# Attention with a pruned context and a gated feed-forward: two PSUM banks for the value products' output, two in place of three for the scores

## The chip, the cores and the metric

One NeuronCore of a Trainium2 chip runs the whole kernel. The metric is the device time of one execution in microseconds (us). TensorE is called PE, VectorE DVE, ScalarE ACT, GpSimd POOL, and SyncE, which issues the transfers, SP.

## What is computed

The input `x` has 8 batches of 512 tokens with 128 channels, in float32. The reference, cut to what matters:

```python
xn  = layernorm(x)
q, k, v = split(xn @ w_attn.T + b_attn)          # 16 heads of 8
att = q @ k.T / sqrt(8), causal
S   = relu(att of head 0), first column and diagonal 0
FF  = cumsum over queries of S, shifted by one    # how far a key is to be forgotten
att = att - FF;  keep = the 102 smallest FF of a row, and the diagonal
att = where(keep, att, -inf)                      # one mask for all 16 heads
attn = (softmax(att) @ v) @ w_proj.T + b_proj
ffn  = sum over 8 experts: gate_e * (relu(xn@wi.T + bi + (xn@A_e.T)@B_e.T) @ wo.T + bo)   # top 2
out  = x + attn + ffn
```

## The kernel before, in words

A first block prepares the weights and the first batch. The second block has 8 steps, one for each batch. A step attends over its own batch (`k`) and at the same time prepares the next one (layer norm, q and k, the forgetting sums of head 0, the search for the 102 smallest, the mask). These preparations are spread over the same time slots.

**Units.** The 512 queries of a batch are four tiles `a` of 128, and tile `a` attends to `a+1` blocks of 128 keys. A unit is the work on up to 512 columns of scores: units 0 to 3 of a step are tile 0 with four heads each, 4 to 11 tile 1 with two heads each, 12 to 27 tile 2 with one head, 28 to 43 tile 3 with one head. So a step has `NU` = 44 units, and there are 352 in all. The text names a unit by its number in the step ("unit 43 of step 3").

**A unit's way.** PE computes the scores into a bank `ps_s` (`score`, line 798). DVE adds the mask, writes the sum to `ar` in SBUF and takes the greatest of each row (`mx`, line 1156). POOL subtracts (line 506). PE transposes the result into a bank `ps_t` (`turn`, line 809). ACT takes the exponential into `pr` (line 657). PE multiplies it with the values into the bank `ps_o` (`weigh`, line 825), for four heads at a time (a group). When all 16 heads of a tile are summed, ACT copies `ps_o` to `out_t` (line 666), PE transposes that (the job `ot0` to `ot3`, line 771), DVE divides by the sum, and the projection follows.

**Order.** Each engine runs one fixed program over the slots `t` = 0, 1, 2 ... In slot `t` PE does the jobs that a table gives for the slot (`fill`: the feed-forward part, the preparations, `ot`, `yt`, `proj`), then `score(t)`, `turn(t-3)` and, where unit `t-4` ends a group, `weigh(t-4)`. DVE does its part of the slot's jobs, the masking of unit `t`, and then a part of the search for the next batch. PE works in order, so that a wait of `score` also holds back the `turn` and `weigh` behind it.

**Rings.** PSUM has eight banks: three for the scores (`NS_RING`), two for the transposes, one for the value products, two for all other jobs (`ps_m`). `score(u)` may begin when unit `u-3` is masked (semaphore `masked`). The first group of a tile may begin when ACT has copied the tile before (semaphore `taken`). DVE adds 1 to `masked` with the instruction that reads the accumulator, at the end of each head.

**The stacks.** The scores are computed in bfloat16 from q and k that are split in three parts, which lie as stacks of 96 rows (`qs`, `ks`), a copy for the current step and one for the next. SP copies the parts into the stacks by 12 transfers of 128 KB in SBUF (line 388, `make_stacks`). The stacks of the next batch overwrite those of the step before, so SP waits for the last score of that step first:

```python
sp.wait_ge(scored, NU * n)      # all scores of the steps before n are computed
```

The first reader of the new stacks is the job `s0` (slot 13 of a step, line 729), which computes head 0 of the next batch: it waits on PE for all 12 transfers. The jobs `ot3` (slot 5 of the next step) and `gate` (slot 43) also play a part below.

Of the kernel before, what the change touches and what calls it, by code (L numbers as in the profile page):

```python
# [23 lines left out]
ACT = mybir.ActivationFunctionType  # L24
AX = mybir.AxisListType.X

P = 128
# [4 lines left out]
NA = T // P  # L32
# [17 lines left out]
OW = 512 // NH  # L50
# [12 lines left out]
OFF = [P * a * (a + 1) // 2 for a in range(NA + 1)]  # L63
FOFF = [sum(T - P * x for x in range(c)) for c in range(NA + 1)]

NS_RING, NT_RING, NM_RING = 3, 2, 2
NA_RING, NP_RING = 6, 6
LAG_T, LAG_P = 3, 4
OUT_LAG, OT_LAG, YT_LAG = 1, 2, 4
# [89 lines left out]
def build(nc, x, w_attn, b_attn, w_proj, b_proj, wi, bi, wo, bo, lora_a, lora_b, gate_w, gate_b, out):  # L159
    ctx = ExitStack()  # L160
    with ctx:
        def sb(name, shape, dt=F32):
            return ctx.enter_context(nc.sbuf_tensor(name, shape, dt))
# [106 lines left out]
        out_t = sb("out_t", [P, T])  # L270
# [4 lines left out]
        def bank(name):  # L275
            return ctx.enter_context(nc.psum_tensor(name, [P, 512], F32))

        ps_s = [bank(f"ps_s{i}") for i in range(NS_RING)]
        ps_t = [bank(f"ps_t{i}") for i in range(NT_RING)]
        ps_o = bank("ps_o")  # L280
        ps_m = [bank(f"ps_m{i}") for i in range(NM_RING)]

        names = ["w_in", "x_in", "const", "w_prep", "scored", "masked", "shifted", "turned", "weighed",
# [8 lines left out]
        weighed, summed, taken = s["weighed"], s["summed"], s["taken"]  # L292
# [13 lines left out]
        def run_block(steps, preps, setup=False):  # L306
# [12 lines left out]
            def wait_full(eng, name, k):  # L319

                eng.wait_ge(m_full, full(name, k))
# [13 lines left out]
            with nc.Block() as block:  # L335
# [185 lines left out]
                def _(act):  # L521
# [78 lines left out]
                    for t in range(end):  # L600
                        k, o = divmod(t, NU)
                        for name, n in plan.at.get(t, []):
# [10 lines left out]
                            elif name in ("q", "k"):  # L613
                                j = ("q", "k").index(name)
# [9 lines left out]
                            elif name[0] == "s":  # L624

                                j = int(name[1])
# [11 lines left out]
                            elif name[0] == "h":  # L638
                                f, j = int(name[1]), int(name[2])
# [4 lines left out]
                            elif name[0:2] == "yt":  # L644
                                a = int(name[2])
# [4 lines left out]
                        if 0 <= u < NU * steps:  # L650

                            a, h0, g = UNITS[u % NU]
# [6 lines left out]
                        for kk in range(steps):  # L659
                            for a in range(NA):  # L660
                                if t == NU * kk + LAST[a] + LAG_P + OUT_LAG:

                                    act.wait_ge(summed, NG * kk + GROUPS * (a + 1))
                                    if NA * kk + a >= 1:
                                        wait_full(act, f"ot{(a + 3) % NA}", kk - (a < 1))
                                    nc.scalar.activation(out_t[:, :], ps_o[:, :], ACT.Identity).then_inc(taken, 1)  # L666
                        for n in range(preps + 1):
                            act_prepares(n, t)

# [1 line left out]
                def _(pe):  # L671
# [141 lines left out]
                    def weigh(u):  # L813
                        k, o = divmod(u, NU)
                        a, h0, g = UNITS[o]
                        group = GROUP_OF[o] % GROUPS
                        pe.wait_ge(weighed, u + 1)
                        if group == 0 and NA * k + a >= 1:
                            pe.wait_ge(taken, NA * k + a)
                        for c in range(a + 1):  # L820
                            for j in range(QUAD):
                                hh = QUAD * group + j
                                unit, at = PLACE_OF[a, hh]
                                at = P * (at + c)
                                last = nc.tensor.matmul(ps_o[OW * j:OW * j + OW, P * group:P * group + P],  # L825
                                                        va[:, k % 2, c, VW * hh:VW * hh + OW],
                                                        pr[:, (NU * k + unit) % NP_RING, at:at + P],
                                                        start=(c == 0), stop=(c == a))
                        last.then_inc(summed, 1)

                    for t in range(end):
                        for name, n in plan.at.get(t, []):
                            fill(name, n)
                        if t < NU * steps:
                            score(t)
                        if 0 <= t - LAG_T < NU * steps:
                            turn(t - LAG_T)
                        if 0 <= t - LAG_P < NU * steps and ENDS_GROUP[(t - LAG_P) % NU]:
                            weigh(t - LAG_P)
# [384 lines left out]
```

## Time and profile before

| | |
|---|---|
| median of 3 runs | 806.2 us (805.84 to 806.38) |
| the profiled execution | 806.93 us |
| its span, first to last instruction | 804.7 us |
| mean granted clock of TensorE | 0.904 of full speed |
| busy: PE, DVE, POOL, ACT | 588.6, 551.2, 439.9, 388.0 us |

The span lacks 2.2 us of the execution's time, which lie before the first and behind the last instruction. No engine is busy for more than 73% of the span, so the time is set by the waits between them, and by different ones in different parts of a step. The times of the rows are counted from the start of the span. A timeline row has the start, the duration, the engine (PEld is the loading of weights, which runs ahead of the PE row with the same line), the line of the kernel and the operation; in brackets stands the idle time before it and what ended it.

### The profile page before, as it was taken

Reading aid. Unit: us, or ns where it says so; the run is one execution under the profiler, and the core shown is the slowest. Engines: PE = TensorE matmul, PEld = TensorE weight load, DVE = VectorE, ACT = ScalarE, POOL = GpSimd, SP = SyncE. Lnnn points to the kernel's source line nnn. Section 1 sums busy time; section 2 is a strip of 40 time slices with the busy share of each in tenths; the row PEclk is TensorE's granted clock in tenths of the full one; section 3 lists DMA queues with packets and bytes.
Section 4 is the critical chain, followed back from the end, with each engine's and each line's share of the span. In section 5 each row is a group of like instructions: output and inputs, shape, how many; then the busy total and the mean of one; then the engine's idle time right before and its main releaser. Section 6 shows DMA issues by size and latency. Waiting matters only on the chain. (4 is left out here: it accounts for less than half of the span.)

```text
span 804.7 us, 16830 instructions
## 1 busy us (share of the span) xinstructions
PE 588.6 (73%) x5478; PEld 401.1 (50%) x5478; DVE 551.2 (69%) x2257; ACT 388.0 (48%) x806; POOL 439.9 (55%) x739
## 2 busy tenths in 40 slices
PE   4133038888688787878887888877787868878995
PEld 2111025466446564555555655655456555656574
DVE  6656426598648984699458985699459964797352
ACT  4124105564446554565456555555446454635543
POOL 4321226547755584547655685558554675439552
PEclk9555559998999999999899999999999999989998
DMA  3502230002500051003400050004200150000000
GB/s 82 67 12 28 27 52 1 1 2 38 69 1 2 7 77 25 1 1 46 62 1 1 20 76 14 2 2 62 32 2 2 33 61 2 1 7 9 1 2 14
DMA packets 27286, 18.98 MB, mean 24 GB/s; under 512 B 5417, under 2 KB 27072, under 8 KB 27200
## 3 DMA queue, kind: packets, MB, share of 16 engines
q1 hardware_dynamic: 27200, 17.91, 15.3%
q8 instruction: 45, 0.74, 0.4%
q14 instruction: 41, 0.34, 0.2%
HBM read 3.22 MB, written 2.10 MB: 7 GB/s over the span
## 5 line engine op out<-in xcount | busy, mean ns | idle before, releaser
L506 POOL TENSOR_SCALAR ar<-ar,mx 128x512 f32<-128x512 f32 (+3 forms) x512 | 285.6, 568 | 284.5 <-DVE mx L1156 283.5
L1156 DVE CUSTOM_DVE_ANT_0 ar<-ps_s,mask 128x512 f32<-128x512 f32 (+3 forms) x512 | 232.6, 484 | 109.0 <-PE ps_s L798 106.2
L657 ACT ACTIVATE pr<-ps_t 128x512 f32<-128x512 f32 (+1 forms) x352 | 192.3, 554 | 136.5 <-PE ps_t L809 132.1
L809 PE MATMUL ps_t<-ident,ar 128*128 128x128 f32 x1280 | 205.5, 279 | 26.1 <-ACT pr L657 13.7
L809 PEld LDWEIGHTS ps_t<-ident,ar 128*128 128x128 f32 x1280 | 157.7, 144 | 70.5 <-POOL ar L506 43.1
L798 PE MATMUL ps_s<-ks,qs 96*128 96x512 bf16 (+3 forms) x512 | 131.1, 309 | 45.4 <-PEq L1195 38.1
L825 PE MATMUL ps_o<-pr,va 128*32 128x128 f32 x2560 | 103.3, 292 | 22.6 <-ACT out_t L666 14.8
L825 PEld LDWEIGHTS ps_o<-pr,va 128*32 128x32 f32 x2560 | 66.3, 114 | 47.4 <-ACT pr L657 32.5
L798 PEld LDWEIGHTS ps_s<-ks,qs 96*128 96x128 bf16 x512 | 46.7, 104 | 75.3 <-issue 57.8
L642 ACT ACTIVATE h<-ps_m,bi_col 128x512 f32<-128x512 f32 x64 | 43.8, 685 | 73.2 <-PE ps_m L756 73.2
L756 PE MATMUL ps_m<-zm,b_t 128*128 128x512 f32 x128 | 70.5, 634 | 5.5 <-ACT h L642 4.5
L596 ACT ACTIVATE junk<-nf,cut 128x384 bf16<-128x384 f32 x64 | 42.2, 662 | 25.2 <-POOL nf L483 13.3
L1106 DVE TENSOR_SCALAR_CACHE_REDUCE nf<-ps_m 128x128 f32<-128x128 f32 (+3 forms) x32 | 15.7, 490 | 41.3 <-PE ps_m L740 40.9
L1156 DVE DVE_READ_ACCUMULATOR2_ANT mx<- 128x1 f32 x512 | 41.9, 82 | 0.0
L752 PE MATMUL ps_m<-xnt,wi_t 128*128 128x512 f32 x64 | 39.5, 702 | 3.0 <-DVE va L1092 3.0
L517 POOL TENSOR_TENSOR hsum<-h 128x512 f32<-128x512 f32 x32 | 40.6, 1268 | 0.0
L756 PEld LDWEIGHTS ps_m<-zm,b_t 128*128 128x128 f32 x128 | 23.0, 199 | 29.9 <-issue 24.8
L951 DVE TENSOR_TENSOR_SCAN ft<-ones,s 128x511 f32<-128x511 f32 (+3 forms) x32 | 26.3, 822 | 13.6 <-POOL s L477 12.1
L771 PE MATMUL ps_m<-ident,out_t 128*128 128x128 f32 x128 | 20.0, 279 | 18.7 <-ACT out_t L666 18.7
L632 ACT ACTIVATE s<-ps_m,not_first 128x512 f32<-128x512 f32 (+3 forms) x32 | 16.6, 525 | 35.0 <-PE ps_m L729 35.0
L729 PE MATMUL ps_m<-qs,ks 96*128 96x512 bf16 (+3 forms) x32 | 10.2, 325 | 31.1 <-DMA ks<-parts 25.1
L765 PE MATMUL ps_m<-wo_t,hsum 128*128 128x128 f32 x256 | 31.2, 275 | 0.0
(172 smaller groups left out, 817.4 us busy)
## 6 DMA issues: line engine op xcount, KB each, us to landing
qs<-parts SPq DMA_DIRECT2D x48, 128.0 KB
ks<-parts SPq DMA_DIRECT2D x48, 128.0 KB
xs<-in_L_attn_x SPq DMA_DIRECT2D x8, 256.0 KB, 5.2
out<-res SPq DMA_DIRECT2D x8, 192.0 KB, 2.1
out<-res SPq DMA_DIRECT2D x8, 64.0 KB, 7.9
ar<-in_L_ffn_wi SPq DMA_DIRECT2D x1, 256.0 KB
ar<-in_L_ffn_wo SPq DMA_DIRECT2D x1, 256.0 KB
ar<-in_L_ffn_lora_B SPq DMA_DIRECT2D x4, 64.0 KB
```

The source lines that it names most:

```text
L506: nc.gpsimd.tensor_scalar(col, col, -1.0, mx[:, t % NA_RING, j:j + 1], ALU.mult, ALU.add)\
L517: nc.gpsimd.tensor_tensor(hsum[:, f, :], h[:, 2 * (f % 2), :], h[:, 2 * (f % 2) + 1, :], ALU.add).then_inc(h_sum, 1)
L596: nc.scalar.activation(junk[:, a - 2, 0:P * (a + 1)], nf[:, OFF[a]:OFF[a + 1]], ACT.Sign, bias=cut[:, a:a + 1], scale=-1.0, accum_out=abov ...
L642: nc.scalar.activation(h[:, 2 * (f % 2) + j, :], m[:, :], ACT.Relu, bias=bi_col[:, f:f + 1])\
L657: nc.scalar.activation(pr[:, u % NP_RING, 0:w], ps_t[u % NT_RING][:, 0:w], ACT.Exp, scale=-1.0)\
L752: nc.tensor.matmul(m[:, :], wi_t[:, P * f:P * f + P], xnt[:, n % 2, :], start=True, stop=False)
L756: last = nc.tensor.matmul(m[:, :], b_t[:, P * f:P * f + P], zm[:, j, :], start=False, stop=True, skip_group_check=(j == 1))
L765: last = nc.tensor.matmul(m[:, P * a:P * a + P], hsum[:, f, P * a:P * a + P], wo_t[:, f, :], start=False, stop=(a == hi - 1 and f == NF - 1))
L798: last = nc.tensor.matmul(ps_s[u % NS_RING][:, w * j:w * j + w], qs[:, k % 2, h0 + j, P * a:P * a + P], ks[:, k % 2, h0 + j, 0:w], start=T ...
L809: last = nc.tensor.transpose(ps_t[u % NT_RING][:, P * j:P * j + P], ar[:, u % NA_RING, P * j:P * j + P], ident[:, :])
L825: last = nc.tensor.matmul(ps_o[OW * j:OW * j + OW, P * group:P * group + P], va[:, k % 2, c, VW * hh:VW * hh + OW], pr[:, (NU * k + unit) ...
L1156: nc.vector.tensor_tensor_reduce(out=ar[:, t % NA_RING, w * j:w * j + w], in0=ps_s[t % NS_RING][:, w * j:w * j + w], in1=mask[:, k % 2, OF ...
```

## The change

Two banks instead of one take the output of the value products, used in turn by tile. To make room for the second, the scores get two banks instead of three. No instruction is added or taken away, and each engine runs the same instructions in the same order as before; only what two kinds of instruction on PE wait for is changed. `score(u)` now waits until unit `u-2` is masked. The first group of a tile now waits for ACT's copy of the tile before the last.

```diff
-NS_RING, NT_RING, NM_RING = 3, 2, 2
+NS_RING, NT_RING, NM_RING, NO_RING = 2, 2, 2, 2
...
-        ps_o = bank("ps_o")
+        ps_o = [bank(f"ps_o{i}") for i in range(NO_RING)]
...
-                                    nc.scalar.activation(out_t[:, :], ps_o[:, :], ACT.Identity).then_inc(taken, 1)
+                                    nc.scalar.activation(out_t[:, :], ps_o[(NA * kk + a) % NO_RING][:, :], ACT.Identity).then_inc(taken, 1)
...
-                        if group == 0 and NA * k + a >= 1:
-                            pe.wait_ge(taken, NA * k + a)
+                        tile = NA * k + a
+                        if group == 0 and tile >= NO_RING:
+                            pe.wait_ge(taken, tile - NO_RING + 1)
...
-                                last = nc.tensor.matmul(ps_o[OW * j:OW * j + OW, P * group:P * group + P],
+                                last = nc.tensor.matmul(ps_o[tile % NO_RING][OW * j:OW * j + OW, P * group:P * group + P],
```

## Rows read from the trace of the kernel before

**Rows 1.** The page, first part: an engine's busy time, share of the span, instructions.

```profile
PE 588.6 (73%) x5478; PEld 401.1 (50%) x5478; DVE 551.2 (69%) x2257; ACT 388.0 (48%) x806; POOL 439.9 (55%) x739
```

**Rows 2.** Waits of PE, whole span: who waited for whom, us, times, longest.

```profile
PE ps_m L729 <- DMA ks<-parts: 25.1, 7, 8.4
...
PE ps_o L825 <- ACT out_t L666: 14.8, 7, 2.3
...
PE ps_s L798 <- DVE mx L1156: 7.2, 8, 0.9
```

**Rows 3.** Timeline of all engines, the start of step 4 (slots 1 to 5).

```profile
464.66 0.08 DVE L1156 DVE_READ_ACCUMULATOR2_ANT mx<- 128x1 f32 x1
...
464.80 0.23 PEld L798 LDWEIGHTS ps_s<-ks,qs 96*128 96x128 bf16 x4 [0.29 <-DVE mx L1156]
...
465.51 0.29 DVE L1156 CUSTOM_DVE_ANT_0 ar<-ps_s,mask 128x128 f32<-128x128 f32 x1
...
468.78 0.15 PEld L798 LDWEIGHTS ps_s<-ks,qs 96*128 96x128 bf16 x2
...
470.26 0.08 DVE L1156 DVE_READ_ACCUMULATOR2_ANT mx<- 128x1 f32 x1
...
471.19 0.59 ACT L666 ACTIVATE out_t<-ps_o 128x512 f32<-128x512 f32 x1
...
471.92 0.43 PE L825 MATMUL ps_o<-pr,va 128*32 128x128 f32 x8 [2.26 <-ACT out_t L666]
472.27 0.42 PEld L771 LDWEIGHTS ps_m<-ident,out_t 128*128 128x128 f32 x4 [0.20 <-issue]
```

**Rows 4.** Timeline of SP: first stack transfers, ends of steps 3, 4 and 5.

```profile
460.13 3.88 SPq L388 DMA_DIRECT2D qs<-parts  x6
...
547.35 3.88 SPq L388 DMA_DIRECT2D qs<-parts  x6
...
636.64 3.88 SPq L388 DMA_DIRECT2D qs<-parts  x6
```

**Rows 5.** Timeline of PE around job s0 of step 4.

```profile
485.99 0.38 PE L729 MATMUL ps_m<-qs,ks 96*128 96x512 bf16 x1 [1.44 <-DMA ks<-parts]
...
487.47 1.13 PE L752 MATMUL ps_m<-xnt,wi_t 128*128 128x512 f32 x2
```

**Rows 6.** Timeline of PE, job s0 of step 5.

```profile
573.59 0.38 PE L729 MATMUL ps_m<-qs,ks 96*128 96x512 bf16 x1 [3.33 <-DMA ks<-parts]
```

**Rows 7.** Line 729 from 200 to 700 us: PE's idle time before it, times.

```profile
  DMA ks<-parts: 16.7, 6
```

**Rows 8.** Timeline at the end of step 3, units 42 and 43.

```profile
458.07 0.10 PEld L798 LDWEIGHTS ps_s<-ks,qs 96*128 96x128 bf16 x1
...
458.81 0.97 PEld L722 LDWEIGHTS ps_m<-gate_t,xnt 128*128 128x128 f32 x8
...
459.28 0.09 DVE L1156 DVE_READ_ACCUMULATOR2_ANT mx<- 128x1 f32 x1
...
459.62 0.18 PEld L798 LDWEIGHTS ps_s<-ks,qs 96*128 96x128 bf16 x1
...
461.63 0.08 DVE L1156 DVE_READ_ACCUMULATOR2_ANT mx<- 128x1 f32 x1
```

**Rows 9.** Timeline at the end of step 0, unit 43's score, unit 41's masking.

```profile
192.08 0.29 PEld L798 LDWEIGHTS ps_s<-ks,qs 96*128 96x128 bf16 x1
...
192.99 0.08 DVE L1156 DVE_READ_ACCUMULATOR2_ANT mx<- 128x1 f32 x1
```

**Rows 10.** The same at the end of step 5.

```profile
636.12 0.18 PEld L798 LDWEIGHTS ps_s<-ks,qs 96*128 96x128 bf16 x1
...
638.13 0.08 DVE L1156 DVE_READ_ACCUMULATOR2_ANT mx<- 128x1 f32 x1
```

**Rows 11.** Windows from s0 to s1, steps 4 and 5: busy times, PEclk, DMA share, GB/s.

```profile
485.99:489.29 3.30, 3.30 (x26) 1.75 (x27) 0.56 (x2) 1.20 (x2) 0.83 (x2) 1.00 0.00 0
573.59:578.52 4.93, 4.93 (x27) 2.17 (x28) 0.57 (x2) 1.20 (x2) 0.83 (x2) 0.67 0.00 0
```

## The prediction

> **What bounds the kernel now.** I read the page first: no engine is full (PE 73%, DVE 69%, [rows 1]), so the question is which wait ends last in each part of a step. Then the waits of PE [rows 2]. Two of them name the buffers of this change: the first value product of a tile waits for ACT's copy `out_t` 7 times, 14.8 us in all, and the scores wait for DVE's masking only 8 times, 7.2 us. Read alone, this says that the value products need the bank and the scores can spare one. The third row, job s0 waiting for the stack transfers, 25.1 us, decides whether that is so.
>
> So next the timeline at the start of a step [rows 3]. All 7 waits for `out_t` are at the first tile of a new step: the group of unit 0 is held until the last tile of the step before is copied (2.26 us, until 471.92). Right behind it in PE's program is job ot3, which transposes that same copy and needs it anyway.
>
> Then SP's timeline [rows 4] and PE at s0. At the end of a step SP waits for unit 43's score and issues the 12 stack transfers at once; s0 waits for the last of them. In step 4 the first is issued at 460.13 [rows 4] and s0 starts at 485.99 [rows 5], 25.86 us later. Of these PE sits idle for the last 1.44 us [rows 5]; in step 5 for the last 3.33 us [rows 6]. Line 729 shows such a wait six times from 200 to 700 us, 16.7 us in all [rows 7], one for each of steps 1 to 6. So the first part of these six steps is set by the transfers, not by PE: whatever PE gains or loses between slot 0 and slot 12 vanishes in this wait, up to its length, and whatever moves **unit 43's score** moves s0 and all behind it.
>
> **The value products' second bank.** It takes away the 2.26 us wait at each start of a step, so that the group of unit 0 (0.35 us from its row to that of ot3, 471.92 to 472.27, [rows 3]) can run while PE waits for the copy. The wait itself goes to ot3. Without any other effect ot3 would start 0.35 us earlier. In six of the seven places the wait for the transfers stands behind it, so it is worth 0 there; where that cover fails it is worth 0.35 us a step. At the other tiles' starts, ot0 to ot2, which need the copy themselves, already come ahead of the next tile's first group in PE's program; nothing is to be had there.
>
> The Trainium skill (Perfetto Trace Analysis, "Matmuls") says that independent groups of matmuls should go through different PSUM banks, so that one's evacuation overlaps the next one's matmuls. By that rule the 14.8 us of rows 2 would be the gain; the trace agrees that the wait is there, but shows the reader of the evacuated data next in line.
>
> **The scores' lost bank: the first-order cost on PE.** `score(u)` must now wait for the masking of unit u-2. I set each score's load in the trace against the end of that masking. In slots 8 to 25 the masking is always done well before, and the ring of two costs nothing. In slots 26 to 43 and 0 to 7, where DVE also searches for the next batch, it is often late. Most of this is not lost: DVE sets the pace there, and a score that comes late still comes before DVE needs it. Tightest is unit 1 of a step: in step 4 the masking it must now follow ends at 464.74 and DVE begins on unit 1 at 465.51 [rows 3]. A wait for `mx` took 0.06 us to release PE (464.74 to 464.80, [rows 3]); four matmuls and their latency take some 0.5 us, so DVE is late by 0 to 0.3 us. At slot 4 the score, before at 468.78, must wait for unit 2's masking, which ends at 470.34 [rows 3], and holds back turn(1), the exponential of unit 1 and with it `out_t`. The score itself is 1.62 us late (470.40 against 468.78); between turn and exponential ACT's other work leaves about 1 us that takes up part of it. My estimate is that `out_t` starts some 0.6 us later than 471.19, and ot3, with the 0.35 us gained, 0.2 to 0.5 us later. In steps 1 to 6 the wait for transfers hides this; in step 7, where nothing is prepared, there is no such wait: **0.4 us**.
>
> **The scores' lost bank: the transfers.** Here the late score is not hidden. At the end of step 3, unit 43's score started loading at 459.62 and SP issued at 460.13. It must now follow unit 41's masking, which ends at 461.71 (461.63 + 0.08): 2.09 us late, with the 0.06 us of release 2.15 [rows 8]. Could PE's own work make it later still? Unit 42's score, before at 458.07, follows unit 40's masking (459.37) at 459.43; from unit 42's score to unit 43's PE needed 1.55 us (turn, and the `gate` job of 0.97 us), so PE is ready at 460.98, before 461.71: DVE decides. The distance is the same at the end of step 5: 636.12 against 638.21, 2.09 us [rows 10]. At the end of step 0 it is 192.08 against 193.07, 0.99 us [rows 9]. The ends of steps 0 to 5 trigger the six waited transfers. DVE's masking of unit 41 comes after the search's last rounds and does not itself move by the late scores; POOL's and ACT's preparations of `parts` are done before.
>
> Sum: 0.99 + 5 x 2.09 + 6 x 0.06 = **11.8 us**. Does it all arrive? s0 starts when the last transfer lands, in all six steps; the transfers take the same time from a later start; PE's arrival at s0 moves by 0.5 us at most, against idle times of 1.44 us and more. Behind s0 PE is busy without a gap (3.30 of 3.30 us, [rows 11]), and then DVE sets the pace on data that come from s0. So each step is longer by the full amount. The Trainium skill (DMA: Bandwidth & Descriptors, "Rules for kernel authors") asks to issue a transfer early and wait for it late; the change issues it later with the wait where it was, and by that rule too the time is longer.
>
> **The clock.** From s0 to s1 the same work takes 3.30 us in step 4, at a granted clock of 1.00 (2.4 GHz), and 4.93 us in step 5, at 0.67, a mean of 2.4 and 1.2 GHz [rows 11]. What PE did before: it was idle for 1.44 us in step 4 and 3.33 us in step 5 [rows 5, 6]. After the change step 4's idle time is near 1.44 + 2.15 - 0.4 = 3.2 us, like that of step 5 before, so I expect the slow stretch there too: 4.93 - 3.30 = **1.6 us**. The others have theirs already; a longer idle time might lengthen it. Bounds: nothing (the slow stretch may even begin while PE is idle), and above a second one in each step, 6 x 1.63 = 9.8 us. I take nothing, since the rows know one only.
>
> **The sum against the profiled execution:** 806.93 + 11.8 + 1.6 + 0.4 = 820.7 us. That execution is 0.7 us above the median shown, so for a median I say **820.0 us**, 1.7% slower.
>
> **Rivals.**
>
> *The second bank pays.* If the 14.8 us of rows 2 were on the path, the time would be 806.2 - 14.8 = 791.4 us. For it: the size of the wait and the ring's good record, 8 waits only. Against: ot3 behind it and the idle time before s0. It decides only if s0 no longer waits for the transfers and ot3 is not held by `out_t`. Chance 4%.
>
> *The late trigger is absorbed*, because the chain from s0 to the end of the step has 2 us of room that a wait elsewhere hides: then 806 us, perhaps 0.35 us less for each start. Against: from s0 to the next step's first issue step 4 took 61.36 us (485.99 to 547.35) and step 5 63.05 us (573.59 to 636.64, [rows 4 to 6]); the 1.63 us that step 4 was quicker just behind s0 [rows 11] were still there at its end, so what happens at s0 comes through. Chance 3%. A part absorbed, as when DVE reaches unit 41 earlier: 811 to 816 us, 7%.
>
> *The scores' waits cost more than the trigger.* PE is late all through slots 26 to 43; if DVE or ACT is held there (feed-forward, turn and exponential stand behind the waiting score), each step loses more: 0.3 us at unit 1 and up to the second slow stretch of 1.63 us, so up to 6 x 1.9 = 11.6 us more, 832 us. For it: many scores wait; against: DVE has room at all but one of them. Chance 16%.
>
> The forecast has the remaining 70%, with a range of its own of 817.5 to 823. A measurement of this kernel tells about 0.2% (1.6 us) from no change: the runs shown spread over 0.07%, and that has to hold on another chip too. Faster: 4%. Same: 3%. Slower: 93%. The range for 8 in 10 is 815.5 to 826: it takes in half of the clock's upper bound and the upper edge of the partial case.
>
> **What the changed kernel's profile would show.** (1) The wait of the value products for `out_t` gone, and ot3 waiting for `out_t` at each start of a step instead, about 2 us. (2) Unit 43's score waiting for `mx`, and SP's first issue 2.1 us closer to the masking of unit 41 and later in its step. (3) From issue to s0 still 26 us, with PE idle there for 3 to 5.3 us in each of steps 1 to 6: some 28 us in all in place of 16.7. (4) Each step about 2.15 us longer from one first issue to the next (step 4: 3.8). (5) The score's waits for `mx` grown from 7.2 us to tens of us, while DVE's busy time and the time from s0 to unit 41's masking stay within 0.5 us (step 4: plus 1.6). If (3) shows a smaller idle time, the trigger is not the cause; if (5) fails, the third rival is right.

## The result, and the profile after

| | before | after |
|---|---|---|
| median | 806.0 us (802.5 to 806.4, 4 runs) | 815.5 us (811.0 to 818.4, 4 runs) |
| the profiled execution | 806.93 us | 818.4 us |
| its span | 804.7 us | 816.2 us |
| granted clock, mean | 0.904 | 0.900 |

The changed kernel is slower: ratio 1.0131, 95% interval 1.0096 to 1.0166. In the later comparisons the kernel before ran between 798.1 and 813.4 us with medians of 804.9, 805.7 and 805.0, so one execution says less than the first three runs let one think. Here and in the experiments a few executions ran in a second, slower state, whatever the kernel; the ratios leave them out, the medians and ranges do not.

The waits of PE in the changed kernel, against [rows 2]:

```profile
PE ps_s L798 <- DVE mx L1157: 48.9, 66, 1.6
...
PE ps_m L729 <- DMA ks<-parts: 32.3, 7, 8.3
PE ps_m L771 <- ACT out_t L666: 19.6, 18, 1.3
...
PE ps_m L771 <- DVE zm L1117: 5.5, 6, 0.9
```

The value products (now line 826) no longer wait for `out_t`: the 14.8 us are gone from the list. The scores' waits have grown from 7.2 to 48.9 us, and the wait of s0 for the transfers, from 25.1 to 32.3 us. The busy times are those of before (PE 588.9, DVE 551.2, against [rows 1]).

The end of step 3, where [rows 8] stood (unit 43's score, the masking it follows, and the transfers that follow it):

```profile
464.19 0.08 DVE L1157 DVE_READ_ACCUMULATOR2_ANT mx<- 128x1 f32 x1
...
464.32 0.10 PEld L798 LDWEIGHTS ps_s<-ks,qs 96*128 96x128 bf16 x1 [0.82 <-DVE mx L1157]
464.33 0.39 PE L798 MATMUL ps_s<-ks,qs 96*128 96x512 bf16 x1 [0.73 <-DVE mx L1157]
...
464.75 1.28 SPq L388 DMA_DIRECT2D qs<-parts  x2
```

Unit 41 is masked at 464.27, the score's load starts 0.05 us later and SP issues 0.43 us after that. Before, SP's first issue came 1.58 us ahead of the end of that masking (460.13 against 461.71, [rows 8]); now it comes 0.48 us behind it. That is the 2.1 us.

The start of step 3, slots 4 and 5, in place of [rows 3]:

```profile
386.46 0.08 DVE L1157 DVE_READ_ACCUMULATOR2_ANT mx<- 128x1 f32 x1
...
386.60 0.39 PE L798 MATMUL ps_s<-ks,qs 96*128 96x256 bf16 x2 [1.40 <-DVE mx L1157]
...
387.36 0.43 PE L826 MATMUL ps_o<-pr,va 128*32 128x128 f32 x8
...
387.96 0.59 ACT L666 ACTIVATE out_t<-ps_o 128x512 f32<-128x512 f32 x1
...
388.70 0.63 PE L771 MATMUL ps_m<-ident,out_t 128*128 128x128 f32 x4 [0.91 <-DVE zm L1117]
```

The wait of 2.26 us for `out_t` is now two others: 1.40 us of the score of unit 4 for the masking of unit 2, and 0.91 us of ot3, which the profile puts down to DVE; `out_t` itself ends only 0.15 us before ot3 starts. From the end of unit 41's masking to ot3 it is 10.79 us (377.91, from its row at 377.83, to 388.70); before, in the same step, it was 10.55 us (372.42 to 382.97). At four more of the seven starts it is the same 10.8 us (at that of step 4 a slow stretch makes it 12.5). The late score costs more than the second bank gains, and the difference is 0.24 us; experiment 1 tells the two apart. The last start, that of step 7, is another matter: 10.47 us against 8.66.

SP's first issue at the ends of steps 3 to 5, in place of [rows 4]:

```profile
464.75 3.89 SPq L388 DMA_DIRECT2D qs<-parts  x6
...
552.43 3.88 SPq L388 DMA_DIRECT2D qs<-parts  x6
...
644.90 3.88 SPq L388 DMA_DIRECT2D qs<-parts  x6
```

PE at s0 of steps 3 to 5, in place of [rows 5, 6]:

```profile
401.30 0.38 PE L729 MATMUL ps_m<-qs,ks 96*128 96x512 bf16 x1 [1.83 <-DMA ks<-parts]
```

```profile
488.99 0.38 PE L729 MATMUL ps_m<-qs,ks 96*128 96x512 bf16 x1 [1.42 <-DMA ks<-parts]
```

```profile
578.61 0.58 PE L729 MATMUL ps_m<-qs,ks 96*128 96x512 bf16 x1 [5.11 <-DMA ks<-parts]
```

And the windows from s0 to s1 of steps 1, 3, 4 and 5 (columns as in [rows 11]; the eighth figure is the granted clock):

```profile
219.93:226.21 6.28, 6.28 (x27) 2.91 (x28) 0.57 (x2) 1.28 (x2) 0.83 (x2) 0.50 0.01 3
401.30:404.60 3.30, 3.30 (x27) 1.74 (x28) 0.56 (x2) 1.20 (x2) 0.83 (x2) 1.00 0.02 5
488.99:492.29 3.30, 3.30 (x26) 1.75 (x27) 0.57 (x2) 1.20 (x2) 0.83 (x2) 1.00 0.01 3
578.61:584.75 6.14, 6.14 (x27) 2.91 (x28) 0.57 (x2) 1.28 (x2) 0.83 (x2) 0.51 0.00 0
```

After the long idle times the whole stretch runs at 1.2 GHz (6.1 to 6.3 us), where before a part of it did (4.9 us); after the two short ones it runs at 2.4 GHz.

**Where the 11.5 us of the two profiled executions lie.** The first issue of a step and the start of s0 cut each step in two:

| step | issue to s0, before | after | s0 to the next issue, before | after |
|---|---|---|---|---|
| 1 | 25.7 | 26.8 | 63.1 | 66.4 |
| 2 | 26.2 | 25.6 | 63.0 | 66.5 |
| 3 | 26.3 | 22.9 | 62.9 | 63.5 |
| 4 | 25.9 | 24.2 | 61.4 | 63.4 |
| 5 | 26.2 | 26.2 | 63.1 | 66.3 |
| 6 | 26.2 | 26.4 | (end of span: 141.8) | (144.9) |

The first issue of step 1 came 0.2 us later. From issue to s0 all six together are 4.4 us *shorter*, from s0 to the next issue the five stretches are 12.6 us longer, and from the last s0 to the end it is 3.1 us: 0.2 - 4.4 + 12.6 + 3.1 = 11.5 us. Step 4 shows the pure price, since neither kernel has a slow stretch behind s0 there: 63.4 against 61.4 us, **2.1 us** unrounded, as predicted. The rest of the 12.6 us, 2.2 us, is the clock: 1.2 to 1.4 us more in each of steps 1, 2 and 5, and 1.6 us less in step 3, which lost its slow stretch.

The 3.1 us after the last s0 have no waited transfer behind them. About 0.9 us is again the slow stretch behind s0 of step 6. The other 2.2 us lie at the start of step 7: from the end of unit 41's masking to the end of unit 4's in the next step it is 9.95 us (735.20 to 745.15) against 7.78 (725.84 to 733.62). The first part of both stretches, up to DVE's start on unit 0 of step 7, before and after:

```profile
725.84:728.25 2.41, 2.10 (x22) 1.24 (x15) 1.22 (x4) 0.77 (x3) 2.23 (x5) 1.00 0.03 7
```

```profile
735.20:738.82 3.62, 3.57 (x43) 2.73 (x44) 1.31 (x4) 0.60 (x1) 2.74 (x5) 0.59 0.00 0
```

In the changed kernel PE waits 1.53 us for unit 41's masking before it scores unit 43, and works at a mean clock of 0.59 behind that. DVE no longer searches in step 7, so nothing hides the lateness. How much of the 2.2 us is the late score and how much the clock isn't shown.

### The profile page after: what moved, and what is told of

Its sections match the earlier page's. It is cut to its first block and busy times, and to the rows that moved or that the text cites. A ratio compares the mean times of both kernels' runs of the same rounds, so it can differ in the third digit from the quotient of the medians.

```text
span 816.2 us, 16829 instructions
## 1 busy us (share of the span) xinstructions
PE 588.9 (72%) x5478; PEld 403.2 (49%) x5478; DVE 551.2 (68%) x2257; ACT 390.9 (48%) x806; POOL 439.8 (54%) x739
## 3 DMA queue, kind: packets, MB, share of 16 engines
q1 hardware_dynamic: 27200, 17.91, 14.8%
## 5 line engine op out<-in xcount | busy, mean ns | idle before, releaser
L798 PE MATMUL ps_s<-ks,qs 96*128 96x512 bf16 (+3 forms) x512 | 132.0, 310 | 87.8 <-DVE mx L1157 48.9
L809 PEld LDWEIGHTS ps_t<-ident,ar 128*128 128x128 f32 x1280 | 160.7, 144 | 33.1 <-issue 12.0
L798 PEld LDWEIGHTS ps_s<-ks,qs 96*128 96x128 bf16 x512 | 44.3, 100 | 134.3 <-DVE mx L1157 78.5
L729 PE MATMUL ps_m<-qs,ks 96*128 96x512 bf16 (+3 forms) x32 | 11.0, 349 | 38.3 <-DMA ks<-parts 32.3
L771 PE MATMUL ps_m<-ident,out_t 128*128 128x128 f32 x128 | 19.9, 278 | 25.1 <-ACT out_t L666 19.6
L952 DVE TENSOR_TENSOR_SCAN ft<-ones,s 128x511 f32<-128x511 f32 (+3 forms) x32 | 26.3, 822 | 13.5 <-POOL s L477 12.0
```

Source lines behind the costliest of these rows:

```text
L798: last = nc.tensor.matmul(ps_s[u % NS_RING][:, w * j:w * j + w], qs[:, k % 2, h0 + j, P * a:P * a + P], ks[:, k % 2, h0 + j, 0:w], start=T ...
L809: last = nc.tensor.transpose(ps_t[u % NT_RING][:, P * j:P * j + P], ar[:, u % NA_RING, P * j:P * j + P], ident[:, :])
```

## The experiments

Each kernel ran beside the kernel before on one chip, in five rounds. Experiments 1 to 4 share one chip, 5, 6, 7 and 10 another, and 8 and 9 a third; kernels of different groups are best compared by their ratio to the kernel before.

**1. Only the lost bank.** The changed kernel with one bank for the value products:

```diff
-NS_RING, NT_RING, NM_RING, NO_RING = 2, 2, 2, 2
+NS_RING, NT_RING, NM_RING, NO_RING = 2, 2, 2, 1
```

> Two banks for the scores, but one for the value products (a PSUM bank lies idle). My theory: the second bank for the value products is worth nothing while the wait for the transfers stands behind it, and at most 0.35 us in the one step without it, so this kernel takes the time of the changed one, 815.5 us, within 1.5 us. Rival (the second bank pays what the wait for out_t shows): 815.5 + 14.8 = 830 us.

Measured: 816.4 us (811.3 to 818.3), ratio 1.0129 (1.0091 to 1.0166), the ratio of the full change. The second bank for the value products is worth nothing that the times can tell, which resolve some 4 us; the rival's 830 us are far off. Its waits of PE:

```profile
PE ps_s L798 <- DVE mx L1157: 44.3, 59, 1.6
...
PE ps_o L826 <- ACT out_t L666: 8.9, 7, 1.3
```

With one bank the wait for `out_t` is back, but with 8.9 us instead of 14.8: the late score of unit 4 has already taken a part of it. The traces are finer than the times. From the end of unit 41's masking to ot3 it is 11.1 to 11.3 us here at the first six starts, 10.8 us in the changed kernel and 10.55 us before. So the second bank is worth some 0.35 to 0.5 us at a start and the late score costs about 0.6 us, both as predicted, and the wait before s0 hides both.

**2. Only unit 43's wait.** The kernel before, three banks for the scores, plus one wait a step:

```diff
+                        if o == NU - 1:
+                            pe.wait_ge(masked, NH * NA * k + HEADS_TO[o - 2])
```

> The kernel before, three banks for the scores and one for the value products, with one more wait on PE: the score of unit 43 of each step also waits until unit 41 is masked, as it must with two banks. All other scores keep the ring of three. My theory: the stack transfers start 2.1 us later in steps 2 to 6 and this alone makes the loss, so 815 us (812 to 820). Rival (the other late scores of slots 26 to 43 and 0 to 7 make it): near 806 us, below 808.

Measured: 816.0 us (811.0 to 819.8), ratio 1.0125 (1.0088 to 1.0162). One wait in each of eight steps makes the whole loss, as far as the medians can tell. Its profile, waits of PE and then the end of step 2:

```profile
PE ps_s L800 <- DVE mx L1158: 21.2, 16, 3.3
...
PE ps_o L827 <- ACT out_t L666: 14.4, 7, 2.2
```

```profile
374.43 0.08 DVE L1158 DVE_READ_ACCUMULATOR2_ANT mx<- 128x1 f32 x1
...
374.63 0.10 PEld L800 LDWEIGHTS ps_s<-ks,qs 96*128 96x128 bf16 x1 [2.05 <-DVE mx L1158]
...
375.07 1.91 SPq L388 DMA_DIRECT2D qs<-parts  x2
```

The scores wait 16 times here and 66 times in the changed kernel, and the time is the same. The 50 other waits cost nothing that can be measured. The wait does not act through the transfers alone, though: at the start of step 7, with no waited transfer behind it, unit 41's masking to unit 4's takes 11.47 us here (7.78 before), part of it at half the clock.

**3 and 4. The transfers taken off the path.** Both kernels with the stack transfers in two halves of heads. The half with head 0 is sent eight units earlier, and s0 waits for that half alone. The main lines of the edit (the rest lays out the columns of q and k and adds the waits of the other engines):

```diff
-                            sp.wait_ge(scored, NU * n)
...
+                        for half in range(2):
+                            lo, hi = (0, NH // 2) if half == 0 else (NH // 2, NH)
...
+                                sp.wait_ge(scored, NU * n - (NH // 2 if half == 0 else 0))
...
-                                sp.dma_start(stack[8 * j:8 * j + 8, into(n), :, :], parts[:, t, part[j], :])\
-                                    .then_inc(stacked, 16)
...
+                                    sp.dma_start(stack[8 * j:8 * j + 8, into(n), lo:hi, :], parts[64 * half:64 * half + 64, t, part[j], :])\
+                                        .then_inc((stacked_0, stacked)[half], 16)
...
-                                pe.wait_ge(stacked, 192 * (nth(n) + 1))
+                                pe.wait_ge(stacked_0, 192 * (nth(n) + 1))
```

> The kernel before with the 12 stack transfers of a step split in two halves of heads (24 transfers of 64 KB): heads 0 to 7 are sent once unit 35 of the step is scored, heads 8 to 15 after unit 43 as before, and job s0, which reads head 0 alone, waits for the first half only. The columns of q and k are laid out so that a half of the heads has 64 partitions next to each other. My theory: PE no longer waits before s0 (16.7 us in six steps) and keeps its full clock behind it (up to 1.63 us in five), so 806 - 25 = 781 us if nothing else takes over, 780 to 792 us. Rival (transfers hidden behind another wait of the same length): 800 to 806 us.

> The changed kernel with the same split of the transfers as before_split. My theory: the change costs time only through the late start of transfers that s0 waits for, so with s0 not waiting for them the cost shrinks to the lateness at slots 1 to 5, 0.2 to 0.5 us a step: 0 to 4 us above before_split. Rival (late scores cost time on their own): 9 us or more above before_split, as between the two kernels without the split.

Measured: before_split 779.0 us (777.8 to 780.4), ratio 0.9683 (0.9650 to 0.9716); after_split 781.3 us (779.7 to 791.8), ratio 0.9705 (0.9672 to 0.9737). The split is worth 26 us where I had expected 25, but not by the parts that I added up. Of the 28.6 us between the spans of the profiled executions, 6.7 us are won before step 0: PE's first score comes at 107.17 us instead of 113.87, and the wait of 8.4 us of the first block's s0, which my sum left out, is gone too. The steps themselves gave 21.9 us. Without the wait the change costs 2.4 us instead of 9.5 to 11, within the 0 to 4 us expected; the intervals of the two overlap, so that even the 2.4 us are not certain. What ended PE's idle time before s0 (now line 733) in before_split:

```profile
its engine sat idle before it (us, times) until:
  ACT h L646: 16.7, 14
  issue: 1.7, 7
  ACT b_t L533: 1.2, 2
  ACT s L636: 1.2, 3
```

No transfer stands there any more, where [rows 7] had 16.7 us. What is left are mostly the waits for ACT before s1 to s3, which the kernel before had as well; that they too come to 16.7 us, over the whole span, is chance.

**5. The second bank with nothing to hide it.** after_split with one bank for the value products, the edit of experiment 1.

> after_split with one bank for the value products instead of two (a bank lies idle). Nothing covers the start of a step any more, since s0 doesn't wait. My theory: the second bank is worth the 0.35 us at each of seven starts, so 2.5 us slower than after_split (781.3): 783.8 us. Rival (the bank is worth the whole wait for out_t): 13.6 us slower, 795 us. Rival (worth nothing at all): 781 us.

Measured: 788.0 us (780.4 to 792.8), ratio 0.9755 (0.9706 to 0.9804). Against after_split (0.9705) this is 0.5% slower, but the intervals overlap: it can't be told whether the bank is worth 0, 2.5 or 6 us here. The whole wait of 13.6 us, a ratio of 0.987, is excluded.

**6 and 7. The reader moved too.** Both split kernels with ot3 one slot later:

```diff
-ATT_JOBS = [(f"ot{a}", LAST[a] + LAG_P + OT_LAG, "dve") for a in range(NA)] + \
+ATT_JOBS = [(f"ot{a}", LAST[a] + LAG_P + OT_LAG + (a == 3), "dve") for a in range(NA)] + \
```

> before_split with job ot3 one slot later in each step (slot 6 for 5; ot0 to ot2 stay). With one bank for the value products the group of unit 0 in slot 4 still waits for out_t, so moving the reader behind it changes nothing: 779 us, within 1.5 us.

> after_split with job ot3 one slot later. My theory: the second bank pays only when the reader that stands behind it is moved too. PE can then do the score, the turn and the products of slot 5 while ACT copies out_t, so the wait of some 2 us at each start of a step is filled for the most part: 5 to 12 us faster than after_split, 769 to 776 us. Rival (DVE or ACT sets the pace there anyway): 780 us or more.

Measured: before_split_ot3 780.2 us (778.5 to 783.0), ratio 0.9679 (0.9644 to 0.9713), as expected. after_split_ot3 784.6 us (780.1 to 786.3), ratio 0.9732 (0.9693 to 0.9772): no gain, and my theory failed. PE at the start of step 3, in the profile of after_split_ot3:

```profile
370.29 0.39 PE L803 MATMUL ps_s<-ks,qs 96*128 96x256 bf16 x2 [0.25 <-DVE mx L1162]
...
371.41 0.66 PE L775 MATMUL ps_m<-ident,out_t 128*128 128x128 f32 x4
...
373.93 0.30 PE L780 MATMUL ps_m<-ident,y 128*128 128x128 f32 x1 [0.85 <-DVE y L1139]
```

ot3 (line 775) no longer waits, but yt3 (line 780), which is now only one slot behind it, waits 0.85 us for the division on DVE.

**8 and 9. Both readers moved.** ot3 and yt3 one slot later:

```diff
-    [(f"yt{a}", LAST[a] + LAG_P + YT_LAG, "act") for a in range(NA)] + \
+    [(f"yt{a}", LAST[a] + LAG_P + YT_LAG + (a == 3), "act") for a in range(NA)] + \
```

> before_split with both readers behind the copy, ot3 and yt3, one slot later. One bank for the value products: the first group of the new step still waits for out_t. 778 to 782 us, as before_split (779.0) and before_split_ot3 (780.2).

> after_split with ot3 and yt3 one slot later. Moving ot3 alone gave nothing: its wait of 0.9 us went to yt3, which waited 0.85 us for the division on DVE. Theory A (the chain ot3, division, yt3 was what held PE; with both moved the second bank pays at last): 0.8 us less in each of seven starts, so 5 us faster than after_split or after_split_ot3 (781.3, 784.6): 775 to 779 us. Theory B (the time there is set by DVE, whose masking the scores of slots 4 to 6 wait for, so that the second bank stays without worth in this kernel): 780 us or more.

Measured: before_split_late2 779.5 us (778.5 to 780.1), ratio 0.9691 (0.9646 to 0.9736); after_split_late2 785.8 us (779.3 to 788.5), ratio 0.9764 (0.9710 to 0.9818). The time is that of theory B: with two banks for the scores, no order of the readers that I tried made the kernel faster, or as fast as before_split. That DVE sets the pace there is argued, not shown by a run of its own. PE at the start of step 3:

```profile
371.85 0.39 PE L803 MATMUL ps_s<-ks,qs 96*128 96x256 bf16 x2 [1.38 <-DVE mx L1162]
373.29 0.39 PE L803 MATMUL ps_s<-ks,qs 96*128 96x256 bf16 x2 [0.25 <-DVE mx L1162]
376.34 0.39 PE L803 MATMUL ps_s<-ks,qs 96*128 96x256 bf16 x2 [0.26 <-DVE mx L1162]
```

The wait of 1.38 us for the masking stands in after_split (1.40) and after_split_ot3 (1.38) as well. Only the waits of ot3 and yt3 are gone, and two of about 0.25 us for the masking have come. What the second bank alone is worth in this order isn't known: the same kernel with one bank was not run.

**10. Another donor.** after_split with three banks for the scores, two for the value products and one for the transposes:

```diff
-NS_RING, NT_RING, NM_RING, NO_RING = 2, 2, 2, 2
+NS_RING, NT_RING, NM_RING, NO_RING = 3, 1, 2, 2
```

> Which ring gives the bank: three for the scores as before, two for the value products, one instead of two for the transposes, with the split transfers. Each turn must wait for the exponential of the unit before it. My theory: the scores keep their lead, but where units follow each other within 0.7 us of PE work the turn waits for an exponential of 0.5 to 0.6 us: 785 to 800 us, slower than after_split. Rival (turns come far enough apart): 776 to 780 us.

Measured: 810.2 us (808.1 to 815.1), ratio 1.0074 (1.0044 to 1.0103), 29 us slower than after_split and beyond my range. The waits of PE in it point to the cause:

```profile
PE ps_t L814 <- ACT pr L661: 69.6, 125, 1.1
```

The transposes now wait for the exponential 125 times; in before_split, with two banks for them, it was 13 times and 15.3 us.

## Why the prediction was right, point by point

**The value products' second bank is worth nothing behind the transfers: shown** by experiment 1, to some 4 us by the times, and by the traces in its parts: 0.35 to 0.5 us at a start, against the 0.35 us of the prediction. I had said that the wait goes to ot3. That was half right: more of it went to the score of unit 4, which now waits 1.4 us for DVE, and ot3 got 0.9 us.

**Late scores are absorbed except at unit 43: shown** by experiment 2 for the loss as a whole. Experiments 3 and 4 leave 2.4 us for all other places, where I had 0.2 to 0.5 us for each of seven starts; five starts had 0.2 us. The last one had more: for step 7, whose start no transfer hides, I had 0.4 us, and it was 2.2 us, the clock's part included. There I had counted the late score at slots 1 to 5 only, and not that unit 43's own late score holds PE at a place where DVE no longer searches.

**The trigger, 2.15 us a step: shown.** Step 4 is 2.1 us longer from s0 to the next issue, experiment 2 reproduces the loss with unit 43's wait alone, and with s0 freed from the transfers most of it is gone. The first of my six terms, 0.99 us at the end of step 0, was too large in the trace: the first issue came 0.2 us later, in an execution whose first score had come 0.5 us earlier.

**The sum was too large**, 13.8 us against 11.5 in the profiled executions and 9.5 between the medians. The median, 815.5 us, lies on the lower edge of my range of 815.5 to 826 and below the 817.5 to 823 of the forecast itself. The step that failed is "the transfers take the same time from a later start". They took 25.7 to 26.3 us in the six steps before and 22.9 to 26.8 us after, 4.4 us less in all; steps 3 and 4 were 3.4 and 1.6 us quicker. Line 388 after the change still moves the same 12 pieces. In the profiles of experiments 1 and 2 the transfers of step 3 were quick as well: s0 came 23.2 and 23.6 us after the first issue, in experiment 2 without any wait for them. So it goes with the late start in these profiles, but for want of more than one profile of the kernel before I can't say that it doesn't also happen there, and why it happens stays open.

**That the sum came so near is in part luck.** By its terms: the trigger 11.1 us (0.7 and 5 x 2.08) instead of 11.8, the clock 3.1 instead of 1.6, step 7 2.2 instead of 0.4, the transfers -4.4 instead of 0, and an execution that began 0.5 us earlier; together 11.5. The quicker transfers made up for two terms that were too small.

**The clock term was near the right size for the wrong reason.** I expected step 4 to get a slow stretch (+1.6 us) since PE would idle for 3.2 us. It idled for 1.42 us, because the transfers were quicker, and kept 2.4 GHz; step 3 idled for 1.83 us and even lost the slow stretch it had. In steps 1, 2 and 5 PE idled for 4.5 to 5.7 us and the slow stretch grew by 1.2 to 1.4 us each, in step 6 (5.3 us idle) by 0.9 us. In sum that is 2.2 us in steps 1 to 5 and 3.1 us with step 6. I had expected 1.6 us. The size was near only by chance: one stretch that I expected did not come, one that was there went, and four grew. The Trainium skill (TensorE: Matmul & The Clock Gate, "HAM oscillation — how this bites in real kernels") describes this pattern, waits for a transfer after which PE starts at half its clock; the trace agrees, with 6.28 us for the work of 3.30.

**The rivals.** That the second bank pays 14.8 us: refuted by experiment 1. That the late trigger is absorbed: refuted by experiment 2, though quicker transfers gave a part of it back in this profile. That the other late scores cost more than the trigger: refuted, at most the 2.4 us of experiments 3 and 4. What I gave as the resolution of a measurement, 0.2%, was too small: executions of the kernel before lie from 0.9% below to 1.1% above their median, and five rounds gave intervals of 0.3 to 0.5% to either side of the ratio.

**By my list of signs:** (1) right for the products, half right for ot3, which waits 0.9 us instead of 2. (2) Right. (3) Wrong in steps 3 and 4: 23.9 us of idle time instead of 28. My list said that a smaller idle time would clear the trigger; that was too strong, since quicker transfers shorten it too. (4) Wrong: from one first issue to the next it is 4.5, 2.9, -2.9, 0.5 and 3.2 us more, 1.6 us on average instead of 2.15, and 0.5 instead of 3.8 in step 4, scattered by the transfers and the clock. (5) Right for the waits and for DVE's busy time. The time from s0 to unit 41's masking changed by 1.3, 1.4, -1.6, 0.0 and 1.2 us in steps 1 to 5, where I had allowed 0.5: these are the slow stretches behind s0. The third rival, which I had tied to this sign, is refuted by experiment 2 all the same.

## What to carry to other kernels

A ring's depth isn't judged by how often its users wait, but by what is triggered behind each of them: here 50 new waits cost nothing that the times can tell, and one a step, the last score before a transfer that someone waits for, cost nearly everything. Before giving a buffer to the longest wait in the list, look one instruction further in the waiting engine's program; if it needs the same result, the wait only moves. And a wait for a transfer is best attacked at the transfer: the kernel before with its transfers split by heads and sent as soon as their half is free takes 779 us, 3.2% less than the kernel before and the fastest of all that ran; of the later edits none beat it.

## What the runs showed of the hardware that I had not expected

The same 12 transfers of 128 KB within SBUF took between 22.9 and 26.9 us from the first issue to the reader's start, nearly all of that range within one kernel (the changed one: 22.9 to 26.8). And after PE had idled for 1.8 and 1.4 us before s0 it went on at 2.4 GHz, while an idle time of 1.99 us in the kernel before (step 3, 4.91 us for the work of 3.30, granted clock 0.65) was followed by a slow stretch, and so was one of 1.53 us at the start of step 7 of the changed kernel (granted clock 0.59). So the length of the idle time alone did not tell what the clock would do.
